# Graph attention over 200,000 edges: gather, softmax and weighted-sum stages replaced by one pass over the edges and a merge stage

## The reference, cut to what matters

```
xh = (h @ W).reshape(n, H, C)
a_src = jnp.einsum('nhc,hc->nh', xh, att_src)
a_dst = jnp.einsum('nhc,hc->nh', xh, att_dst)
alpha = jax.nn.leaky_relu(a_src[src] + a_dst[dst], 0.2)
amax = jax.ops.segment_max(alpha, dst, num_segments=n)
alpha = jnp.exp(alpha - amax[dst])
denom = jax.ops.segment_sum(alpha, dst, num_segments=n)
out = jax.ops.segment_sum(xh[src] * (alpha / denom[dst])[:, :, None], dst, num_segments=n)
```

## Time and profile before

| | us |
|---|---|
| median of three runs (16518.1 to 16524.77) | 16523.53 |
| the profiled execution | 16444.79 |
| its span, first to last instruction | 16443.0 |

### The profile page before, as it was taken

The page is one execution under the profiler, slowest core; times in us unless marked ns, Lnnn a source line. Parts: engine busy times, 40 slices in busy tenths (PEclk is TensorE's granted clock), DMA queues, the critical chain, the costliest instruction groups (busy, mean ns, idle before and its releaser), DMA issues. The chain is left out here.

```text
span 16443.0 us, 107327 instructions
## 1 busy us (share of the span) xinstructions
PE 6230.6 (38%) x29851; PEld 5397.4 (33%) x29852; DVE 3125.4 (19%) x4383; ACT 824.4 (5%) x1247; POOL 9777.0 (59%) x9860
## 2 busy tenths in 40 slices
PE   3333333333333444420000003985555656433333
PEld 2333333333333333320000002863555654333333
DVE  3222221000011111210000013663111112311111
ACT  1000000000000000000000001012000000100000
POOL 2666666666666666667777742003666663466666
PEclk8555555555555555555555556986555556655555
DMA  2111111111111222223333322423222222222122
GB/s 87 48 47 48 47 48 44 49 48 48 49 46 53 56 55 54 58 68 103 99 99 101 97 28 62 146 106 99 85 82 83 88 81 79 75 54 55 53 53 53
DMA packets 568146, 1124.62 MB, mean 68 GB/s; under 512 B 220819, under 2 KB 364378, under 8 KB 541572
## 3 DMA queue, kind: packets, MB, share of 16 engines
q0 software_dynamic: 307488, 624.42, 15.0%
q1 hardware_dynamic: 260616, 499.73, 9.0%
HBM read 904.32 MB, written 218.95 MB: 68 GB/s over the span
## 5 line engine op out<-in xcount | busy, mean ns | idle before, releaser
L680 POOL DMA_INDIRECT work<-rows_a,index x4704 | 4663.9, 991 | 2270.4 <-issue 1540.1
L750 PE MATMUL psum<-onehot,work 128*128 128x80 f32 x12544 | 2762.0, 418 | 4410.6 <-DMA work<-rows_a,index 3032.2
L750 PEld LDWEIGHTS psum<-onehot,work 128*128 128x128 f32 x12544 | 2675.5, 327 | 4488.3 <-issue 4470.1
L680 POOL DMA_INDIRECT work<-rows_b,index x3136 | 3167.2, 1010 | 1618.4 <-issue 1073.4
L1190 POOL DMA_INDIRECT work<-attention_rows,index x1568 | 1608.9, 1026 | 611.7 <-issue 557.6
L750 PE MATMUL psum<-onehot,regionB 128*128 128x80 f32 x6272 | 1177.6, 353 | 730.9 <-issue 462.0
L750 PEld LDWEIGHTS psum<-onehot,regionB 128*128 128x128 f32 x6272 | 1112.0, 267 | 790.7 <-issue 751.8
L845 DVE TENSOR_TENSOR regionA<-regionA,psum 128x80 f32 x1176 | 273.2, 232 | 5257.0 <-remote 2816.2
L764 PE MATMUL psum<-onehot,regionB 128*4 128x80 f32 (+1 forms) x6272 | 1024.1, 329 | 461.6 <-issue 461.3
L764 PEld LDWEIGHTS psum<-onehot,regionB 128*4 128x4 f32 (+1 forms) x6272 | 946.3, 210 | 493.0 <-issue 474.5
L182 POOL COPY work<-regionB 128x500 f32 (+1 forms) x75 | 45.3, 603 | 1684.2 <-DVE regionB L561 1684.2
(11 more groups left out here) (253 smaller groups left out, 4510.5 us busy)
## 6 DMA issues: line engine op xcount, KB each, us to landing
gathered_rows<-work SPq DMA_DIRECT2D x98, 1088.0 KB
work<-gathered_rows SPq DMA_DIRECT2D x98, 1088.0 KB, 4.9
regionB<-in_edge_attr SPq DMA_DIRECT2D x195, 512.0 KB
work<-rows_a,index POOLq DMA_INDIRECT x4704
work<-rows_b,index POOLq DMA_INDIRECT x3136
work<-attention_rows,index POOLq DMA_INDIRECT x1568
x_transposed<-regionA SPq DMA_DIRECT2D x75, 250.0 KB, 6.0
rows_a<-regionC SPq DMA_DIRECT2D x50, 250.0 KB
```

Of the source, the lines that this page charges most:

```text
L680: pool.indirect_dma_start(rows3[h][:, t, :], None, table, bass.IndirectOffsetOnAxis(ap=net.index[:, k, h * ST + t:h * ST + t + 1], axis=0) ...
L750: last = nc.tensor.matmul(bank_of(h, q, 0), msgs3[h][:, t, 0:D], onehot[:, h * ST + t, :], start=(k == 0), stop=(k == GT - 1))
```

## The change

The three attention stages before `gat_output` and the gather stage become two stages, `gat_pass` and `gat_merge`.

- `gat_pass` gathers the 1568 tiles once into a ring of three pairs in region C; nothing goes back to HBM. In each of 49 turns, for the pair's 32 tiles: ScalarE copies the scores out, TensorE transposes them (edges along the row, tile and head down the partitions), VectorE scans forward and backward for the maximum of each segment inside a tile, and a scan over the 32 tile ends carries it across tiles. The destination scores reach the edges by 16 transposes of the one-hot matrix and 16 small products. The running maximum that crosses from pair to pair rescales the first node's sums (`alpha`). ScalarE takes two exponentials, VectorE multiplies rows by weights, TensorE sums rows and weights over groups of 4 tiles with a window of 64 nodes, VectorE adds them in. The sums of turn n-1 are placed inside turn n.
- `gat_merge` loads the projected features (`XHT`, new in HBM, written by `Project`), adds each node's own term and divides.
- `Project` makes two more products a chunk, two more PSUM copies and one less activation, and one more store. `Sage` loses the counts' scan. `prepare` makes segment flags and tile chains in HBM (8 stores of 784 KB in pieces of 512 bytes, 5 small ones), 32 more transposes, and no longer clears `segment_starts`. `gat_output` loses the division.

```diff
+GT4 = 4
+W4 = 64
...
-                lambda: gat_gather(net),
-                lambda: gat_softmax(net),
-                lambda: gat_begin(net),
-                lambda: aggregate(net, "agg3", extra="attention", follow=Shares(net, "shares")),
+                lambda: gat_pass(net),
+                lambda: gat_merge(net),
                 lambda: gat_output(net),
```

POOL and ScalarE in a turn (n counts turns, s is the ring slot, k the parity):

```diff
+                def gather(j, n, s, k, f3, f2):
+                    pool.wait_ge(index_ready, r * (NIT + 2) + j + 1)
+                    pool.wait_ge(summed[1], n + 1)
+                    for t in range(2 * HALF):
+                        pool.indirect_dma_start(
+                            ring[s][:, t, :], None, net.XH,
+                            bass.IndirectOffsetOnAxis(ap=net.index[:, k, t:t + 1], axis=0)).then_inc(gathered[s], 16)
...
+                    act.wait_ge(chained, n + 1)
+                    for g in range(2 * GQ):
+                        x = S.copy(cuts[:, g * P:(g + 1) * P]..., own_table[:, bass.ds(at[g], W4)]...)
+                    act.wait_ge(gathered[s], (r * fills3[s] + f3) * 512 + 512)
+                    act.wait_ge(scored, n + 1)
+                    S.copy(heads4(score_of[k]), ring[s][:, :, D:D + H]).then_inc(taken, 1)
+                    for f in range(4):
+                        act.wait_ge(flips, n * 4 + f + 1)
+                        S.copy(flipped[:, f * 512:(f + 1) * 512], bank(2 + f % 2)).then_inc(flips_copied, 1)
+                    S.copy(own_edge, bank(4 + k)[:, 0:256]).then_inc(own_copied, 1)
+                    S.activation(alpha, change, ACT.Exp).then_inc(alpha_ready, 1)
+                    act.wait_ge(scored, n + 3)
+                    S.activation(ring[s][:, :, D:D + H], u4[:, 0], ACT.Exp)
+                    S.activation(own_p, u[:, P:2 * P], ACT.Exp).then_inc(weighed, 1)
```

TensorE's order in a turn:

```diff
+                    T.transpose(score_t, score_of[k], net.ident[:, :]).then_inc(score_ready, 1)
+                    for g in range(2 * GQ):
+                        t = T.transpose(bank(1)[:, g * 2 * H:(g + 1) * 2 * H], cuts[:, g * P:(g + 1) * P], ...)
+                    pe.wait_ge(onehot_ready, r * (NIT + 1) + j + 1)
+                    for f in range(4):
+                        pe.wait_ge(flips_copied, n * 4 + f + 1)
+                        for q in range(4):
+                            t = T.transpose(bank(2 + f % 2)[:, q * P:(q + 1) * P], onehot_flat[k][...], net.ident[:, :])
+                    sums_of(pe.snap(n - 1), (s + 2) % 3, 1 - k, 0)
+                    pe.wait_ge(ends_ready, n + 1)
+                    T.matmul(bank(1)[0:H, 64:128], sel, ends, start=True, stop=True)
...
+                    for q in range(HALF):
+                        m = T.matmul(bank(4 + k)[:, q * 16:(q + 1) * 16], flipped[:, q * P:(q + 1) * P], blocks[...])
+                    m.then_inc(own_ready, 1)
+                    T.matmul(bank(1)[:, 192:256], sel_t, carried, start=True, stop=True).then_inc(spread, 1)
+                    T.transpose(max_e, back, net.ident[:, :]).then_inc(max_turned, 1)
+                    T.matmul(bank(1)[:, 256:257], head_select(net), alpha, start=True, stop=True)
+                    sums_of(pe.snap(n - 1), (s + 2) % 3, 1 - k, 1)
```

```diff
+                    dve.wait_ge(weighed, n + 1)
+                    V.tensor_tensor(ring[s][:, :, D + H:XW], heads4(own_p), last[k]..., ALU.mult)
+                    for h in range(2):
+                        x = ring[s][:, h * HALF:(h + 1) * HALF, :]
+                        V.tensor_tensor(by_head, by_head, x[:, :, D:D + H]..., ALU.mult).then_inc(message[h], 1)
+                    if not first:
+                        add(dve.snap(j - 1), dve.snap(n - 1), 1, before)
+                    compare(1 if first else dve.snap(j + 1), 1 - k)
```

`gat_merge`, per chunk of 500 nodes:

```diff
+                V.tensor_tensor(net.col(Cc, c), net.col(Cc, c), net.psum[:, at + 512:at + 512 + CH], ALU.mult)
+                V.tensor_tensor(net.col(A, c), net.col(A, c), net.col(Cc, c), ALU.add)
+                V.tensor_tensor(net.col(A, c), net.col(A, c), net.psum[:, at:at + CH], ALU.mult)
```

More of the change, by code:

```diff
@@ L42 @@
 W = 80
-EPP = EP // P
 H = 4
@@ L608, in aggregate @@
     A, Cc = net.A, net.C
-    attention, edges = extra == "attention", extra == "edges"
-    width = XW if attention else D
+    edges = extra == "edges"
+    width = D
     S = 2
@@ L627, in aggregate @@
     staged = NIT - 1 + ahead
-    high = [P, H if attention else P]
+    high = [P, P]
     dense = follow and follow.dense
@@ L635, in aggregate @@
     onehot_ready = name("onehot")
-    gathered = name("gathered") if attention else [net.pool_sem() for _ in range(S)]
+    gathered = [net.pool_sem() for _ in range(S)]
     summed = name("summed")
@@ L642, in aggregate @@
     piled = name("piled") if extra == "count" else onehot_ready
-    ready = relued if edges else message if attention else gathered
+    ready = relued if edges else gathered
     with nc.Block() as block:
@@ new lines, in _, with gather @@
+        @block.gpsimd
+        def _(pool):
+            if edges:
+                pool.wait_ge(lists, 48)
+            R = pool.value_load(net.rounds[0:1, 0:1], min_val=1, max_val=256)
+            with pool.Fori(0, R) as r:
+                def gather(i, k):
+                    n = pool.snap(r * NIT + i)
+                    pool.wait_ge(index_ready, r * staged + i + 1)
+                    for h in range(S):
+                        if edges:
+                            pool.wait_ge(message[h], n + 1)
+                        else:
+                            pool.wait_ge(summed[h], n * SG + SG)
+                        pool.sem_inc(moved, 1)
+                        for t in range(ST):
+                            pool.indirect_dma_start(
+                                rows3[h][:, t, :], None, table,
+                                bass.IndirectOffsetOnAxis(ap=net.index[:, k, h * ST + t:h * ST + t + 1], axis=0)
+                            ).then_inc(gathered[h], 16)
+                each_pair(pool, gather)
@@ L686, in _ @@
         @block.sync
         def _(sp):
-            if not (attention or edges):
+            if not edges:
                 if dense:
@@ L1196, in _ @@
         @block.vector
         def _(dve):
[L1198 to L1203 removed]
+            for h in range(2):
+                dve.sem_inc(added[h], 1)
+            dve.sem_inc(message[1], 2)
+            dve.sem_inc(scored, 2)
@@ new lines, in gat_merge @@
+def gat_merge(net):
+    nc = net.nc
+    A, B, Cc, V = net.A, net.B, net.C, net.nc.vector
+    s = {k: net.sem(f"gm_{k}") for k in ("xh", "turned", "step", "packed", "back", "rows", "spread", "merged",
+                                         "shift", "wide", "select", "sum")}
+    both = net.work[0:SUB, 0:NSUB * 2 * H]
+    both3 = both.rearrange("p (t f) -> p t f", f=2 * H)
+    spare = net.work[0:SUB, 800:800 + NSUB * H].rearrange("p (t h) -> p t h", h=H)
+    total = net.work[0:SUB, 1200:1200 + NSUB * H].rearrange("p (t h) -> p t h", h=H)
+    rows = [net.work[0:2 * H, 1600 + k * 512:1600 + k * 512 + CH] for k in range(2)]
+    shifted = net.small[0:H, 60:60 + 2 * H]
+    select = [net.wtmp[0:2 * H, 668 + k * P:668 + (k + 1) * P] for k in range(2)]
+    with nc.Block() as block:
```

1063 lines of the change are left out of this document (567 added, 496 removed).

## The result

Against the kernel before on one chip the change took 16290.21 us (median of 4 runs, 16275.13 to 16321.94) in place of 16524.15: a ratio of 0.9861, interval 0.9849 to 0.9873. It is faster, by 234 us where 1288 were forecast, and outside the range. The experiments ran in six sets on six different chips; whether one of them is the chip of the comparison is not known.

| where | before, us | changed, us | ratio and interval |
|---|---|---|---|
| the comparison | 16524.15 | 16290.21 | 0.9861 (0.9849 to 0.9873) |
| second set | 16513.79 | 16283.19 | 0.9861 (0.9841 to 0.9880) |
| third set | 16445.29 | 16206.01 | 0.9852 (0.9835 to 0.9868) |
| fifth set | 16506.86 | 16302.73 | one run each |
| first, fourth set | 15212.44, 15283.32 | not run unedited | |

What follows compares the result with a forecast made beforehand. It took POOL's gathering to bound the gather stages and the new pass, at 44.6 us a turn. Terms -3700 + 2277 + 125 - 25 + 15 + 20 = -1288 took 16523.5 to 15235 us; range 15050 to 15600.

Steps and rivals of the forecast that it cites:

- the other chain of a turn: In the pass: TensorE and VectorE's alternating work takes 43 us a turn, under 44.6, so POOL never waits.
- rival A: In the pass: that TensorE and VectorE work sets the turn, 46 to 56 us, kernel 15305 to 15795 us; 27%.
- the 71: In the pass: only from 71 us a turn on would that work make the kernel slower than before.
- POOL's turn: In the pass: 32 gathers with issue 40.7 us, plus what VectorE holds up, 44.6 us a turn (40.7 to 47.5).
- Rival B: In the pass: every two-SBUF-operand VectorE operation stops POOL for its length, 50 us a turn, kernel 15500 us; 8%.
- the rate of 0.52 us per us: In the second aggregation: POOL loses 0.52 us per us of VectorE comparison; applied to the pass's wide operations.
- Pass, 2277: New attention pass: launch, clears, 49 turns of 44.6 us (2185) and the uncovered last turn sum to 2277 us.
- Merge, 125: New merge stage: loading, 25 chunks at 3.2 us and 10 for half clock, together 125 us (95 to 170).
- Output stage, -25: gat_output: loses a product of 1.1 to 2 us in each of 25 chunks, -25 us (-40 to 0).
- Preparation, +20: Preparation: 32 transposes and 6.4 MB in small pieces, partly where clearing the old table was, +20 us (-5 to +60).
- Project, +15: Project: two more products a chunk, minus one activation, mostly in TensorE's idle time, +15 us (0 to +60).
- Sum, -1288: Whole kernel: 3700 us of old attention stages removed, the new stages and small terms added, net -1288 us.

Runs made afterwards that it cites:

- one_gather_2: Changed kernel with 1 gather per pair of halves in the pass in place of 32: 14635.46 us with gaps; the same edit without gaps, 13555.49 us.
- paced_half: Changed kernel plus one POOL wait: a pair's second sixteen gathers start after the own-term products; 14078.90 us beside 15224.71 before, ratio 0.9247, without gaps.
- after_third: Profile of the unedited changed kernel in the third set: 16213.74 us, where the kernel of before took 16430.84 to 16469.12.
- agg1_long: Kernel of before, TensorE's second-aggregation loop written out for two turns per iteration: 15216.58 us beside 15212.44 without gaps, 16462.57 beside 16445.29 with.

## Why the prediction was wrong

**The failed step** is "the other chain of a turn": "POOL never waits if the rest of a turn takes less than 44.6". The rest takes 33.6 us by itself (one_gather_2, at a granted clock of 0.64), and still POOL waited 26 us a turn. The step added TensorE's operations at the durations that their rows show, as if they could run beside gathers at that speed. On the chips with gaps they can't: after 79 to 83 records of a turn the next come singly, up to 2.8 us apart, and the rest of the turn's work waits until the gathers end. On the chips without gaps they can, and POOL's turn of 43.9 us is the bound, as forecast. The sign the prediction set for rival A, POOL idle in each turn until TensorE's sums, is what the profile shows, but not by A's mechanism (register loads and handovers), and past its 46 to 56 us; it stayed short of the 71 at which the kernel would be slower.

**It could be read beforehand.** The edges stage of before has the same two engines side by side, and I took no row of it. Its groups, and the timeline of one stretch:

```profile
L764 PE MATMUL psum<-onehot,regionB 128*128 128x80 f32 x3136 | 750.0, 411 | 461.6 <-issue 461.3
L750 PE MATMUL psum<-onehot,regionB 128*128 128x80 f32 x3136 | 749.3, 412 | 643.0 <-issue 462.0 <-ACT regionB L661 179.1 <-DVE regionA L845 1.9
```

```profile
12517.03 3.62 PE L750 MATMUL psum<-onehot,regionB 128*128 128x80 f32 x16
12520.44 1.56 PE L764 MATMUL psum<-onehot,regionB 128*128 128x80 f32 x6
...
12553.84 0.29 PE L750 MATMUL psum<-onehot,regionB 128*128 128x80 f32 x1 [2.51 <-issue]
12556.64 0.29 PE L750 MATMUL psum<-onehot,regionB 128*128 128x80 f32 x1 [2.51 <-issue]
```

That is 923 us of idle time by issue in one stage. Here 118 records lie between POOL's restart (12495.08) and the first gap; at the other restarts of the stage that are followed by a fresh run of gaps it is 90 to 258 records, 23 to 65 us. So neither a number of records nor a time is a limit that holds for both stages. The new pass has 198 records a turn, three times those of an aggregation. What these rows could not tell is that other chips show none of it.

Term by term, with the chip with gaps first (the changed kernel's profile) and the one without second (paced_half):

- *POOL's turn, 44.6:* 66.6 and 43.9. The part that VectorE holds, forecast at 3.9, is (1.068 - 0.944) x 32 = 4.0 on the chip without gaps, where everything overlaps; on the other the mean is 983 ns and little is held. Rival B, gathers held in full, falls, and the rate of 0.52 us per us stands. The Trainium skill, GPSIMD Engine Reference, section Key points, names the contention that this shows, not its rate.
- *Chain, 43:* 66.6 with gathers on a chip with gaps, 33.6 with one gather a pair; with all gathers on a chip without gaps it stays under POOL's 43.9.
- *Pass, 2277:* 3334 and 2247.
- *Merge, 125:* 145 and 147. TensorE was granted 0.50, its level of 1.2 GHz, throughout, and busy for 135.6 us, where I had put only the first chunks, 10 us of the sum, at half clock.
- *Output stage, -25:* -36 (216 to 180).
- *Preparation, +20:* +16 (first gather at 294.0, then at 309.7).
- *Project, +15:* the three aggregations took 54 us more, inside the bound of 60; 15 in the closer pair (after_third).
- *Sum, -1288:* -234 by the medians; -1146 of 15225 with paced_half, 7.5% where 7.8% were forecast. There the three terms from pass to output are 2573 us; a kernel of before with only a loop written out (agg1_long) has 3707 for the stages that these replace, where the profile I forecast from has 3916. So the forecast's pass fits that chip, 2277 and 2247, but its saving was counted against slower stages of before: the middle was to save 1323 us and saved 1134. That the total came so near is in part luck, since a chip without gaps was not what I read.

## What to carry to other kernels

A stage's cost is not the longest of its engines' sums unless the trace shows those engines busy side by side at that density; look for the stage where they already are, and read its idle time by "issue" and "remote" first. When work is moved beside a stream of gathers, look at how many instructions TensorE has in each stretch of gathers, not only at how long they take: 64 a turn had 1.6 us of gaps here, 96 had 192, and 198 had over a thousand. And run both kernels on several chips: here the same two kernels differ by 1.4 or 1.5% wherever there are gaps, and the change, with one wait added that never held, by 7.5% on a chip without.

## What the runs showed of the hardware

- In the comparison and on three of the six chips behind it TensorE, beside POOL's gathers, did 79 to 83 records at full speed in a turn of the pass and 90 to 258 in the edges stage, and then single ones 0.7, 1.4, 2.1 or 2.8 us apart, until about 5 us after POOL had stopped. Its signals to VectorE and POOL came up to 27 us late in that time. POOL's gathers themselves were held as well, with TensorE idle: 2165 us for 1568 in place of 1979. On the other three chips none of this occurs.
- Neither a seventeenth of the bytes, nor a shorter or a longer loop body changes it. What inside the chip does it, and why on some chips only, is not settled; that POOL's issuing or its descriptors are the cause is what is left over, not shown, and the part of the profiler's recording is untested.
- TensorE's code in the pass is written out for six turns and had to be brought in anew: 111 transfers of 16 KB in the changed kernel, 15 in the kernel of before. On a chip without gaps the turn of 43.9 us is POOL's own, so they cost nothing; by the Trainium skill, Runtime: NRT & Kernel Launch, section Instruction fetch mechanics, such blocks are streamed and mostly hidden, and the trace agrees. What shows of it is a wait by issue of 0.9 to 1.4 us before L1365 once in six turns, at the loop's return, in one_gather and one_gather_2, where POOL is not the bound. The page of the changed kernel:

```profile
q8 instruction: 111, 1.82, 0.0%
```
